# Attention values spread over the first query tiles, four gate pieces moved to tiles 6 to 9, and three pieces of the next layer put into the last tile

## What is computed

```python
xn = _layernorm(x)
# attention, one head of 128, rotary positions on half of it, causal
q, k, v = rope(xn @ wq), rope(xn @ wk), xn @ wv
p = softmax(q @ k.T - 1e30 * mask)
a = (p @ v) @ wo
# feed-forward on the same xn, ternary weights, 512 wide
h = silu(tlin(xn, w1)) * tlin(xn, w2)
h = gelu(tlin(h, h1))
h = gelu(tlin(h, h2))
x = x + a + tlin(h, w3)
```

## Time and profile before

| | us |
|---|---|
| median of 3 executions (lowest, highest) | 279.69 (279.57, 280.02) |
| the profiled execution | 278.56 |
| its span, first to last instruction | 276.4 |
| busy: TensorE, VectorE, ScalarE, GpSimd | 259.1, 214.7, 193.8, 100.8 |
| projections of the second layer end, values begin | 108.9 |
| attention tiles | 112.5 to 209.1 |
| two layers of 512x512 on TensorE | 209.15 to 264.40 |
| mean granted clock of TensorE | 0.998 |

### The profile page before, as it was taken

How to read it: one execution, slowest core, us unless ns; L and a number is a source line. 1 busy time by engine, 2 the same in 40 slices (tenths; PEclk the granted TensorE clock), 3 DMA queues, 4 the chain that set the end, 5 groups by cost and what they waited for, 6 DMA issues and landing times.

```text
span 276.4 us, 5402 instructions
## 1 busy us (share of the span) xinstructions
PE 259.1 (94%) x1794; PEld 168.2 (61%) x1798; DVE 214.7 (78%) x729; ACT 193.8 (70%) x471; POOL 100.8 (36%) x130
## 2 busy tenths in 40 slices
PE   7899899999977699799999999999999999999993
PEld 2379845456653445657778777778794444444483
DVE  6977489999997689589999878877943766666684
ACT  1487489885665579678756799999674877777730
POOL 9314000000000068988884389889771000000000
PEclk9999999999999999999999999999999999999999
DMA  7700000000000280400000000000000000000005
GB/s 201 208 13 2 2 0 4 1 0 0 2 2 0 85 373 2 152 2 4 0 2 0 2 0 0 5 0 0 2 0 2 0 0 0 4 1 0 0 9 148
DMA packets 8287, 8.51 MB, mean 31 GB/s; under 512 B 1729, under 2 KB 7362, under 8 KB 7746
## 3 DMA queue, kind: packets, MB, share of 16 engines
q1 hardware_dynamic: 7826, 7.84, 8.8%
q10 hardware_dynamic: 432, 0.30, 0.4%
HBM read 7.09 MB, written 1.05 MB: 29 GB/s over the span
## 4 chain that ended last, share of the span: by engine, by line
PE 65%; DVE 25%; ACT 4%; issue 3%; DMA 2%; SPq 0%; DVEq 0%; ACTq 0%
PE PS L861 10%; PE PS L862 10%; PE PS L819 10%; PE PS L799 9%; PE PS L810 4%; PE PS L491 3%; DVE arena L1564 3%; PE PS L510 3%; DVE arena L1551 2%; DVE arena L1596 2%; PE PS L776 2%; PE PS L777 2%; DVE arena L1587 2%; DMA x<-L_attn_x 2%; DVE arena L1652 1%
## 5 line engine op out<-in xcount | busy, mean ns | idle before, releaser
L861 PE MATMUL PS<-arena 128*128 128x512 f16 x128 | 48.6, 379 | 0.6 <-issue 0.6
L862 PE MATMUL PS<-arena 128*128 128x512 f16 x128 | 48.6, 379 | 0.0
L1869 DVE TENSOR_TENSOR arena<-arena 128x512 f32<-128x512 f32 x32 | 22.2, 693 | 19.5 <-ACT arena L1264 19.5
L799 PE MATMUL PS<-arena 128*128 128x512 f32 (+3 forms) x80 | 32.1, 531 | 0.0
L1263 ACT ACTIVATE arena<-PS,arena 128x512 f32<-128x512 f32 x32 | 22.0, 688 | 13.2 <-PE PS L862 13.2
L1324 POOL CAST arena<-arena 128x512 f16<-128x512 f32 x2 | 1.3, 648 | 72.7 <-ACT x L1125 72.7
L1316 POOL TENSOR_TENSOR arena<-arena 128x256 f32<-128x256 f32 x32 | 21.5, 672 | 15.6 <-DVE arena L1808 13.2
L1237 ACT ACTIVATE arena<-PS,lnt 128x512 f32<-128x512 f32 (+3 forms) x40 | 24.9, 634 | 1.9 <-DVE lnt L1823 1.7
L1317 POOL TENSOR_TENSOR arena<-arena,small 128x256 f16<-128x256 f32 (+1 forms) x36 | 23.8, 660 | 2.8
L1816 DVE TENSOR_REDUCE mxb<-PS 128x1 f32<-128x512 f32 (+3 forms) x40 | 22.1, 601 | 1.6 <-PE PS L801 1.6
L861 PEld LDWEIGHTS PS<-arena 128*128 128x128 f16 x128 | 12.5, 98 | 15.7 <-issue 0.7
(11 more groups left out here) (283 smaller groups left out, 633.3 us busy)
## 6 DMA issues: line engine op xcount, KB each, us to landing
arena<-h_T SPq DMA_DIRECT2D x2, 1024.0 KB, 5.8
x<-L_attn_x SPq DMA_DIRECT2D x4, 256.0 KB, 4.6
arena<-cos SPq DMA_DIRECT2D x1, 1024.0 KB, 4.8
arena<-sin SPq DMA_DIRECT2D x1, 1024.0 KB, 6.9
out<-arena SPq DMA_DIRECT2D x4, 256.0 KB, 2.3
arena<-w_T SPq DMA_DIRECT2D x3, 256.0 KB, 3.1
con<-shape_constants ACTq DMA_DIRECT2D x1, 192.0 KB, 3.3
w1e<-L_ffn_W SPq DMA_DIRECT2D x1, 128.0 KB
```

The lines of the kernel that those rows point to most:

```text
L799: i = mm(PS[:, k, 0:cnt * P], qT1[:, t * P:(t + 1) * P], kT1[:, c * P:(c + cnt) * P], start=True, stop=not last)
L861: mm(bank(u % 8), wH[:, k, m * P:(m + 1) * P], sH[:, k, cols], start=(k == 0), stop=False)
L862: i = mm(bank(u % 8), wL[:, k, m * P:(m + 1) * P], sL[:, k, cols], start=False, stop=(k == HT4 - 1))
L1869: v.tensor_tensor(RP[m], FP[m], high, ALU.subtract).then_inc(rest_ready, 1)
```

## The change

Of the four chunks of values only chunk 0 stays ahead of tile 0. Chunks 1, 2 and 3 are computed in passes 0, 1 and 1 of the loop, in PSUM banks 5, 6 and 3 instead of 0, 5 and 1, and all four are copied out by VectorE. Tiles 0 and 1 no longer have gate pieces; tiles 6 to 9 have a third one, placed late. `ACT_HIGH` goes from 12 to 10, so VectorE casts 22 pieces and ScalarE 10. Of the first 512x512 layer, pieces 0, 1 and 2 (24 products) are placed in the last pass, ahead of `weighted` of the groups 0, 2 and 3 of tile 15, and the wait for all results of attention becomes a wait of piece 7 alone. The waits of scores, transposes and gates are set to the new banks.

```diff
-ACT_HIGH = 12
+ACT_HIGH = 10
...
-        PER = NU // NT
-        assert PER == 2
-        GATE_EARLY = [range(PER * t, PER * t + (2 if t < FULL else 1)) if t < NT else () for t in range(NT + 1)]
-        GATE_LATE = [range(GATE_EARLY[t].stop, PER * t + PER) if t < NT else () for t in range(NT + 1)]
-        GATE_BANK = [3 if u % PER and u // PER < FULL else 6 for u in range(NU)]
+        EARLY_GATES, LATE_GATES = (0, 0, *(2,) * (FULL - 2), *(1,) * (NT - FULL), 0), (*(0,) * 6, 1, 1, 1, 1, 0, 0, *(1,) * (NT - FULL), 0)
+        GATES_AT = [sum(EARLY_GATES[:t] + LATE_GATES[:t]) for t in range(NT + 1)]
...
+        GATE_BANK = [3 if u % 2 and u < GATES_AT[FULL] else 6 for u in range(NU)]
...
+        VALUE_BANK = (4, 5, 6, 3)
...
             def values(c):
-                b = (4, 0, 5, 1)[c]
-                pe.wait_ge(*((xt2_act, c + 3) if c < 2 else (skip_act, 2 * c + 2)))
+                b = VALUE_BANK[c]
+                pe.wait_ge(xt2_act, 4 if c else 3)
+                if c == 1:
+                    pe.wait_ge(skip_act, 6)
+                if c >= 2:
+                    pe.wait_ge(rope_dve, 8)
...
-            for c in range(4):
-                values(c)
+            values(0)
...
-                if u == 0:
+                if u < 2:
                     pe.wait_ge(w16_ready, 4)
+                    pe.wait_ge(v1_act, u + 3)
...
+            AMONG = (0, 2, 3)
+
+            def layer_piece(layer, u):
...
+                if u >= 8:
+                    pe.wait_ge(read, u - 7)
+                elif layer:
+                    pe.wait_ge(g1_act, 8 + u + 1)
+                elif u == 0:
+                    pe.wait_ge(w16_ready, 2 * NWT)
+                    pe.wait_ge(p_ready, len(SCORE_BANK))
+                elif b == 4:
+                    pe.wait_ge(pt_act, len(SCORE_BANK))
+                elif b == 6:
+                    pe.wait_ge(hA_ready, NU)
+                elif b == 7:
+                    pe.wait_ge(pv_read, NT)
...
+                if t < 2:
+                    values(t + 1)
                 for u in GATE_EARLY[t]:
                     gated(u)
                 for k, g in enumerate(groups):
                     if k + 1 == len(groups):
                         for u in GATE_LATE[t]:
                             gated(u)
+                    if t == NT and k in AMONG:
+                        layer_piece(0, AMONG.index(k))
                     weighted(t - 1, *g)
...
-            pe.wait_ge(w16_ready, 2 * NWT)
-            pe.wait_ge(pv_read, NT)
...
+                if t == 1:
+                    values(3)
...
-            act.wait_ge(v1_act, 2)
-            for c in range(2, 4):
-                act.wait_ge(v1_done, c + 1)
-                f(V1[:, 4 * c:4 * c + 4, :].rearrange("p n d -> p (n d)"), bank((4, 0, 5, 1)[c]), ACT.Copy).then_inc(v1_act, 1)
...
-            for c in range(2):
+            def values(c):
                 dve.wait_ge(v1_done, c + 1)
-                v.tensor_copy(V1[:, 4 * c:4 * c + 4, :].rearrange("p n d -> p (n d)"), bank((4, 0)[c])).then_inc(v1_act, 1)
+                v.tensor_copy(V1[:, 4 * c:4 * c + 4, :].rearrange("p n d -> p (n d)"), bank(VALUE_BANK[c])).then_inc(v1_act, 1)
...
                 if t == 0:
 
+                    values(0)
...
+                if t < 2:
+                    values(t + 1)
                 for u in GATE_EARLY[t]:
                     gate(u)
...
+                if t == 1:
+                    values(3)
                 for u in GATE_LATE[t]:
                     gate(u)
```

More of the change, by code:

```diff
@@ L332, in program @@
         NU = HT4 * T // ZC
[L333 to L337 removed]
+        EARLY_GATES, LATE_GATES = (0, 0, *(2,) * (FULL - 2), *(1,) * (NT - FULL), 0), (*(0,) * 6, 1, 1, 1, 1, 0, 0, *(1,) * (NT - FULL), 0)
+        GATES_AT = [sum(EARLY_GATES[:t] + LATE_GATES[:t]) for t in range(NT + 1)]
+        GATE_EARLY = [range(u, u + n) for u, n in zip(GATES_AT, EARLY_GATES)]
+        GATE_LATE = [range(u + e, u + e + n) for u, e, n in zip(GATES_AT, EARLY_GATES, LATE_GATES)]
+        assert GATE_LATE[-1].stop == NU
+        GATE_BANK = [3 if u % 2 and u < GATES_AT[FULL] else 6 for u in range(NU)]
         GATE_AFTER = [max([w for w in range(u) if GATE_BANK[w] == GATE_BANK[u]], default=None) for u in range(NU)]
+        VALUE_BANK = (4, 5, 6, 3)
         V_RUNS = [(b, s0, min(26, S - s0)) for b, s0 in zip((7, 6, 0, 1, 2), range(0, S, 26))]
@@ L806, in turn_round @@
                 pe.wait_ge(p_ready, gi + 1)
+                if gi < 2:
+                    pe.wait_ge(v1_act, gi + 1)
                 if gi >= 2:
@@ L821, in weighted @@
                     i.then_inc(pv_done, 1)
+            AMONG = (0, 2, 3)
+            def layer_piece(layer, u):
+                wH, wL, sH, sL, done, read = ((h1H, h1L, hAH, hAL, g1_done, g1_act), (h2H, h2L, hBH, hBL, g2_done, g2_act))[layer]
+                ch, m, b = u // HT4, u % HT4, u % 8
+                cols = slice(ch * BANK, (ch + 1) * BANK)
+                if m == 0:
+                    (pe.wait_ge(low_ready, 4 * ch + 4) if layer else pe.wait_ge(gate_low, NU // 4 * (ch + 1)))
+                if u >= 8:
[11 more added lines that the diff above has]
+                    pe.wait_ge(pv_read, NT)
+                for k in range(HT4):
+                    mm(bank(b), wH[:, k, m * P:(m + 1) * P], sH[:, k, cols], start=(k == 0), stop=False)
+                    i = mm(bank(b), wL[:, k, m * P:(m + 1) * P], sL[:, k, cols], start=False, stop=(k == HT4 - 1))
+                i.then_inc(done, 1)
             for t in range(NT + 1):
@@ L828, in _ @@
                     turn_round(t - 1, *g)
[L829 to L837, removed]
+                if t == 0:
+                    pe.wait_ge(rope_dve, 6)
+                    pe.wait_ge(sums_ready, 2)
+                    mm(PS[:, 7, 0:2], ones, sums, start=True, stop=True).then_inc(sums_done, 1)
+                if t < 2:
+                    values(t + 1)
                 for u in GATE_EARLY[t]:
@@ L846, in _ @@
                         turn_round(t - 1, *groups[k + 2])
-            pe.wait_ge(w16_ready, 2 * NWT)
-            pe.wait_ge(pv_read, NT)
-            for layer, (wH, wL, sH, sL, done, read) in enumerate(((h1H, h1L, hAH, hAL, g1_done, g1_act), (h2H, h2L, hBH, hBL, g2_done, g2_act))):
-                for ch in range(4):
-                    cols = slice(ch * BANK, (ch + 1) * BANK)
-                    (pe.wait_ge(low_ready, 4 * ch + 4) if layer else pe.wait_ge(gate_low, NU // 4 * (ch + 1)))
-                    for m in range(HT4):
-                        u = 4 * ch + m
-                        if u >= 8:
-                            pe.wait_ge(read, u - 7)
-                        elif layer:
-                            pe.wait_ge(g1_act, 8 + u + 1)
-                        for k in range(HT4):
-                            mm(bank(u % 8), wH[:, k, m * P:(m + 1) * P], sH[:, k, cols], start=(k == 0), stop=False)
-                            i = mm(bank(u % 8), wL[:, k, m * P:(m + 1) * P], sL[:, k, cols], start=False, stop=(k == HT4 - 1))
-                        i.then_inc(done, 1)
+                if t == 1:
+                    values(3)
+            for layer in range(2):
+                for u in range(4 * HT4):
+                    if layer or u >= len(AMONG):
+                        layer_piece(layer, u)
             for n in range(NT):
```

9 lines of the change are left out of this document (7 added, 2 removed).

## The result

The changed kernel takes 276.74 us (median of 4 executions, 276.38 to 277.21) against 279.63 for the kernel before in the same comparison: 0.990 of it, with a 95% interval of 0.9864 to 0.9935. The forecast was 277.3. What separates these two numbers lies ahead of the changed code, and has to be cleared first.

A forecast was written before the change was run, and what follows sets the result against it. TensorE and VectorE were both taken as full, with TensorE idle only in the front and last pass. Front 1.2 plus last pass 1.2 gave 2.4 us off 279.69, so 277.3; own range 276.4 to 277.9, wider range 275.3 to 278.9.

The forecast's parts named there:

- The front of tiles 0 and 1: Start of attention: maxima of tile 2 at 115.45 instead of 120.55, TensorE idling 0.8 us for the exponentials.
- first rival: Whole kernel: only TensorE's work counts and VectorE catches up, 4.7 us gained, 275.0 us; chance 0.14.
- VectorE carries the lead and spends it: Tiles 2 to 8: VectorE is full; its lead of 4.7 us at tile 6 falls to 3.0 at tile 8.
- TensorE is held at the late pieces: Tiles 6, 7 and 8: TensorE waits 0.5 to 0.9 us each for VectorE to free a bank.
- The last pass: Tile 15 and start of the layers: two TensorE gaps, 0.5 and 0.7 us, are filled, gaining 1.2 us.
- Behind tile 10 all work is as before: After tile 10: work is unchanged, so the front's gain of 1.2 us stays.
- TensorE alone: Whole kernel: only TensorE's work counts, casts are cheaper and VectorE catches up, 4.7 us gained, 275.0 us; chance 0.14.
- VectorE losing more: Two late casts before piece 16 meet GpSimd (2 x 0.45), front gives only 0.3, 278.2 us; chance 0.2.
- The last pass giving nothing: Last pass: f16 pieces delay copies or GELU's late start reaches TensorE, 1.2 us gained alone, 278.5 us; chance 0.08.
- The slow one: Tiles 6 to 9: VectorE's result and TensorE's late piece wait for each other, 3.2 us slower, 282.9 us; chance 0.06.

The follow-up runs named there:

- e12: Changed kernel with VectorE reducing the first group of scores twice in tiles 3, 4 and 5; 279.44 us, 1.000 of the kernel before.
- e6: Changed kernel with ScalarE instead of VectorE casting the early gate pieces of tiles 7 to 9; 277.01 us, 0.991 of the kernel before.
- e1: Kernel before with only the three layer pieces in the last pass and the later wait for attention results; 277.89 us, 0.994 of the kernel before.
- e3: Changed kernel with one layer piece in the last pass instead of three; 276.94 us, 0.990 of the kernel before.
- e4: Changed kernel with the third gate pieces in tiles 7 to 10 instead of 6 to 9; 276.84 us, 0.991 of the kernel before.
- e8: Changed kernel with VectorE's checks of the weights moved behind the bias of the next pass; 276.74 us, 0.989 of the kernel before.
- e9: Changed kernel with third gate pieces in tiles 7 to 10 and weight checks behind the next pass's bias; 275.26 us, 0.985 of the kernel before.

## Why the prediction was right, step by step

- **The front of tiles 0 and 1.** Forecast: maxima of tile 2 at 6.57 behind the start of the values, one wait of 0.8 for the exponentials. Measured 6.69 and 0.8. The 3.5 us that would stay if TensorE alone counted, a side figure of the prediction and the base of its first rival, was 0.5 too large: the window that gave 4.3 us idle holds waits in pass 3 that the change leaves in place (by starts 0.2 ahead of the second gate piece and 0.4 at 120.57). So 1.9 us were lost to VectorE, not 2.3. The forecast did not rest on that figure.
- **VectorE carries the lead and spends it.** Forecast: 4.7 us ahead at tile 6, maxima of tile 8 at 141.6 - 108.88 = 32.7, scores of tile 9 at 36.8. Measured: 25.46 before against 20.89, so 4.6 ahead; 32.97; 37.13. Two terms in between were wrong and nearly cancel, which is luck. Tile 6 lengthened by 0.91 us instead of 0.46: its late piece cost 1.5 and not 1.19, as its cast met GpSimd (0.55 instead of 0.29). Tile 7 lengthened by 0.91 instead of 1.19: its late piece cost 1.17 as forecast, but its first cast no longer met GpSimd (0.29 at 139.19, against the 0.55 that it took before, in the row below). The net of both, with 0.1 lost at the start, is 0.3 us at tile 8, and 0.2 of it is left in the front's 1.03 against 1.2. That TensorE's own work does not set the pace is shown by e12. That VectorE's work is only 0.1 to 0.2 us ahead of the chain through the tanh is shown by e6, and was not in the forecast.

```profile
141.89 0.55 DVE L1808 CAST arena<-arena 128x256 f16<-128x256 f32 x1
```

- **TensorE is held at the late pieces.** Forecast 0.5 to 0.9 each in tiles 6, 7 and 8; measured 0.48, 0.76, 0.66, each ended by VectorE, 1.9 in all.
- **The last pass.** Forecast 1.2 from two gaps, measured 1.3 (e1), and one piece suffices (e3, within 0.1). GELU's later start cost nothing that shows: TensorE is busy without a gap from 203.35 to 263.05.
- **"Behind tile 10 all work is as before"** held for this change: 1.03 at tile 10, 1.03 at tile 12, 1.02 at tile 15. It is no rule: in e4 a lead of 1.6 us at tile 12 was 1.2 at tile 15.
- **Rivals.** TensorE alone (275.0): falls with e12 and with the three waits. VectorE losing more because both late casts ahead of piece 16 meet GpSimd (278.2): one of the two did, in tile 6; the other missed it by 0.09 us, so this rival was near. The last pass giving nothing (278.5): falls with e1. The slow one, in which result and late piece wait for each other, did not happen in tiles 6 to 9, where VectorE never waited for the product. Its mechanism (a late piece between a result and the next maxima) is what cut e4's gain in tiles 12 and 13.
- The timed median moved by 2.9, the sum was 2.4 and the profiles say 2.3 (at the last operation 2.32: 1.02 from the front and 1.30 from the last pass, where 1.2 and 1.2 were forecast). The front came out short and the last pass long, so the closeness of the sum is in part luck. The 0.6 between the medians' 2.9 and the profiles' 2.3 is not explained by any trace; it may lie in how many of the few timed executions ran a low clock ahead of the values.

## What to carry to other kernels

Say one engine gains time because idle time at the start is removed, and the work taken out there must be done later, in a stretch where a second engine is full too. Then the first engine keeps only what the second can follow. Add up gains and extra work for both, and find the first place where a buffer makes one wait for the other. A lead can also be lost behind the change: look at the next pass in which an unrelated operation stands between a result and what the next step waits for, and move it behind (e4 and e8 alone gave 0.16 and 0.43 us, together in e9 1.06). To measure steps of a few tenths, count from an event just ahead of the first changed instruction to one just behind the last.
